# One transformer layer with a mixture of experts on one core: experts that add into the output, a split routing, and a reordered front and attention

## The chip, the core and the metric

The kernel runs on one core of one Trainium2 chip. The core has five engines with a queue of instructions each: TensorE (PE, with its weight loads shown as PEld), VectorE (DVE), ScalarE (ACT), GpSimd (POOL) and SyncE (SP), which here only issues DMAs. The engines wait for each other through semaphores. The metric is the device time of one launch in microseconds; smaller is better.

## The reference

The input is 2048 token numbers. Everything is float32, and the kernel keeps that accuracy by splitting operands of a matmul into an upper and a lower part (`hi`, `lo`) and adding three products.

```python
h = ternary_weights(tok_weight)[x]                       # embedding, T=2048, C=256
# attention: 16 heads, three branches, mixed by a gate over the sequence
a1 = attn(q, k1, v1, causal=True)                        # latent keys and values
idx = top_k(x @ w_imp, 64); sel = x[sort(idx)]           # 64 most important tokens
a2 = attn(q, ks(sel), vs(sel), causal=False)             # selected
a3 = attn(q, kw, vw, causal=True)                        # "window"
h = h + (g0*a1 + g1*a2 + g2*a3) @ w_proj
# experts: E=8, top 2 per token, F=512
logits = layernorm(h) @ router_w.T
w1, w2, i1, i2 = sparsemixer(logits)                     # mask by 2*jitter, softmax, pick
for e in range(8):
    y = (silu(x @ w_gate[e].T) * (x @ w_up[e].T)) @ w_down[e].T
    out = out + dense_w[:, e:e+1] * y
h = h + out
```

## The kernel before

The program is a row of stages, each a block at whose end all engines meet: embed (0 to 121 us), project (to 304), select (to 384), attend (to 2221), mix (to 2345) and experts (to the end).

**Project** runs a list of tasks, `front_tasks()`, merged from several streams so that they alternate. A task has a part on PE and one on DVE or ACT, and for stored results one on ACT (`st_hi`, rounding up, L584), POOL (`st_lo`, the rest, L451) and SP (two stores, L399). A `rank` task compares one block of 128 tokens' importance with all others on DVE (three instructions that read `row_all`, L682 to L685) and counts on PE with 17 matmuls of one column (L505, L508). The third phase holds 16 ranks, the `q` tasks, and `v` and `kn` tasks.

**Select** turns the ranks into 64 one-hot columns (`hot`, DVE L917), gathers the selected tokens by matmuls `U`·`hot` on PE (L846) and projects them (L853). `frs` is the flag times each token's `rstd`, multiplied into the one-hot columns.

**Attend** walks 84 units per head (a unit is 512 queries by 128 keys). Per unit: PE makes scores, DVE adds the mask on diagonal units (L1736), ACT makes `prob` and its rounded form `p_hi`, POOL or DVE subtracts them to `p_lo` (L1418, which engine is set by the list `LO_DVE`), and PE multiplies both with the values four units later (L1599, L1601). PE takes them in the fixed order of units. In heads 0 to 11 preparation for later heads is woven in: tasks `prep` whose products are turned on DVE (L1666, L1676), summed on POOL (`turn_sum`, L1400), rounded up on ACT (L1467) and lowered on POOL (`turn_low`, L1408) or, for one part of a `q` task, on DVE (L1661). The values of the next head are split once per head and kind (ACT, then POOL L1430); `SPLIT_W` says at which unit. `FINISH` says at which units DVE finishes the previous head's output.

**Mix** multiplies the heads' outputs with the projection, adds the residual, takes a layernorm and the router logits, and then routes: two gates on DVE (L2021 to L2044), positions of tokens by scans and matmuls, a one-hot code of each token's slot (L2077 to L2092) and a matmul that inverts it (L1907), giving `slot_tok` (which token lies in a slot) and `slot_w` (its weight). It also writes two accumulators in DRAM: `acc0` with the residual `h1`, `acc1` with zeros.

**Experts** takes 23 tiles of 256 slots. POOL per tile `i`: four `h_lo` subtractions (L2177), after the first two indirect gathers for tile `i+2` (L2159), and at the end two indirect scatters that add the rows of tile `i-1` into `acc0` and `acc1` (L2169). The first scatter of a tile waits for the first of the tile before, the second for the second. Slots with no token point to dummy rows behind the 2048. When all are in, SP loads both accumulators (L2146), DVE adds them (L2326), and SP stores the output (L2149).

## Time and profile before

| | us |
|---|---|
| median of 3 runs | 2634.81 (2633.99 to 2637.43) |
| the profiled execution | 2636.5, its span 2634.8 |
| PE, DVE, POOL, ACT busy | 2237.9, 1877.2, 1758.6, 1720.0 |
| mean granted clock of PE | 0.92 of full speed |
| project, select, attend, mix, experts, end | 183, 80, 1837, 124, 268, 22 |

The times of a stage are read by where one block's instructions end and the next one's begin. "End" is what follows the landing of the last scatter. Of the page's forty slices PE is at 9 tenths in those of attend and lower before and after; the busy share of an engine over the whole span says little about the stages outside attend.

### The profile page before, as it was taken

To read this page: it belongs to the slowest core of one execution; us is meant where nothing else is said; L and a number is where in the kernel's file an instruction comes from. 1 tells how busy PE (TensorE), PEld (TensorE's weight loads), DVE (VectorE), ACT (ScalarE), POOL (GpSimd) and SP (SyncE) were. 2 spreads that over 40 slices of the span, in tenths; PEclk is the share of its full clock that TensorE was granted. 3 is DMA by queue.
4 is the path that set the end of the run, shared out by engine and by line. 5 is a ranking of instruction groups with operands and counts; after the bars stand their busy time and mean duration, and the time that the engine had idled before them with its cause. 6 is when DMAs were issued, how large, how long until landed. Compare 5 with 4: busy or idle time off the path is not lost. (4 is left out here: it accounts for less than half of the span.)

```text
span 2634.8 us, 37397 instructions
## 1 busy us (share of the span) xinstructions
PE 2237.9 (85%) x11394; PEld 1863.9 (71%) x11394; DVE 1877.2 (71%) x3720; ACT 1720.0 (65%) x3574; POOL 1758.6 (67%) x1544
## 2 busy tenths in 40 slices
PE   0178578999999999999999999999999994839885
PEld 0165437887878788787878878788888883728885
DVE  2656467687887878787787878788888873555553
ACT  3433216787877878777787777788888883216663
POOL 4154516778787877878787787877878774017884
PEclk9975569999999999999999999999999997759998
DMA  9767726345252434425342542322412203426776
GB/s 380 327 204 236 224 62 166 75 91 133 62 137 74 93 86 96 119 75 134 77 93 76 107 111 63 94 43 55 80 34 55 44 16 87 140 83 189 194 197 169
DMA packets 199860, 314.81 MB, mean 119 GB/s; under 512 B 95915, under 2 KB 130219, under 8 KB 186731
## 3 DMA queue, kind: packets, MB, share of 16 engines
q1 hardware_dynamic: 189947, 298.23, 40.6%
q0 software_dynamic: 9712, 14.18, 2.9%
q8 instruction: 91, 1.49, 0.2%
q14 instruction: 110, 0.90, 0.1%
HBM read 210.20 MB, written 101.75 MB: 118 GB/s over the span
## 5 line engine op out<-in xcount | busy, mean ns | idle before, releaser
L1418 POOL TENSOR_TENSOR p_lo<-prob,p_hi 128x512 fp32r<-128x512 f32 (+3 forms) x1072 | 1232.6, 1169 | 396.6 <-ACT p_hi L1502 368.4
L1500 ACT ACTIVATE prob<-ps_s 128x512 f32<-128x512 f32 (+4 forms) x1344 | 727.2, 541 | 380.8 <-DVE ps_s L1736 208.8
L1502 ACT ACTIVATE p_hi<-ps_s 128x512 fp32r<-128x512 f32 (+3 forms) x1344 | 726.3, 540 | 1.6
L1634 DVE TENSOR_REDUCE max_part<-ps_x 128x1 f32<-128x512 f32 x744 | 506.7, 687 | 108.5 <-PE ps_x L1546 98.2
L1632 DVE CUSTOM_DVE_ANT_0 ps_x<-ps_x,before 128x128 f32<-128x128 f32 x496 | 244.0, 492 | 30.5 <-PE ps_x L1546 22.0
L1599 PE MATMUL ps_o<-p_hi,v_lat 128*128 128x512 f32 (+3 forms) x640 | 240.3, 376 | 26.0 <-POOL p_lo L1418 25.9
L1599 PE MATMUL ps_o<-p_hi,v_win 128*128 128x512 f32 (+3 forms) x640 | 238.0, 372 | 2.7 <-POOL p_lo L1418 2.7
L1601 PE MATMUL ps_o<-p_lo,v_lat 128*128 128x512 f32 (+3 forms) x640 | 237.8, 372 | 0.0
L1601 PE MATMUL ps_o<-p_lo,v_win 128*128 128x512 f32 (+3 forms) x640 | 235.2, 367 | 0.0
L1418 DVE TENSOR_TENSOR p_lo<-prob,p_hi 128x512 fp32r<-128x512 f32 (+1 forms) x208 | 207.7, 999 | 10.8 <-ACT p_hi L1502 10.7
L1736 DVE TENSOR_TENSOR ps_s<-ps_s,mask_kq 128x128 f32<-128x128 f32 x512 | 150.2, 300 | 74.2 <-PE ps_s L1518 65.6
L1599 PEld LDWEIGHTS ps_o<-p_hi,v_lat 128*128 128x128 f32 x640 | 122.3, 191 | 55.7 <-POOL p_lo L1418 32.9
L1695 DVE TENSOR_TENSOR raw_o<-ps_o,low_sum 32x512 f32<-32x512 f32 x192 | 131.4, 684 | 26.2 <-ACT low_sum L1482 19.7
L1599 PEld LDWEIGHTS ps_o<-p_hi,v_win 128*128 128x128 f32 x640 | 121.5, 190 | 30.3 <-POOL p_lo L1418 8.2
L2159 POOL DMA_INDIRECT xg<-x_scratch,slot_tok x46 | 51.7, 1124 | 130.4 <-POOLq L1755 119.8
L1514 PE MATMUL ps_s<-head_first 97*128 97x512 f32 (+1 forms) x320 | 123.3, 385 | 16.0 <-POOL v_lat L1434 8.2
L1601 PEld LDWEIGHTS ps_o<-p_lo,v_lat 128*128 128x128 f32 x640 | 123.3, 193 | 19.2
L1601 PEld LDWEIGHTS ps_o<-p_lo,v_win 128*128 128x128 f32 x640 | 122.4, 191 | 17.8
L1514 PE MATMUL ps_s<-q_hi,kw_hi 97*128 97x512 f32 (+1 forms) x320 | 121.0, 378 | 6.3 <-ACT p_hi L1502 5.8
L1546 PE MATMUL ps_x<-k_hi,head_first 96*128 96x512 f32 (+2 forms) x320 | 119.3, 373 | 4.1 <-DVE turned L1677 1.8
L1514 PE MATMUL ps_s<-q_hi,k_hi 99*128 99x512 f32 (+1 forms) x320 | 120.0, 375 | 0.3 <-ACT p_hi L1502 0.3
L1517 PE MATMUL ps_s<-head_first,k_hi 96*128 96x512 f32 (+1 forms) x320 | 119.7, 374 | 0.0
(433 smaller groups left out, 5823.6 us busy)
## 6 DMA issues: line engine op xcount, KB each, us to landing
raw<-in_experts_w_dram SPq DMA_DIRECT2D x23, 1536.0 KB
wbuf<-in_tok_weight_dram SPq DMA_DIRECT2D x16, 2000.0 KB, 16.9
head_first<-kw_scratch SPq DMA_DIRECT2D x72, 256.0 KB, 5.0
kw_scratch<-st_hi SPq DMA_DIRECT2D x48, 256.0 KB, 2.3
kw_scratch<-st_lo SPq DMA_DIRECT2D x48, 256.0 KB, 3.0
q_scratch<-st_hi SPq DMA_DIRECT2D x48, 256.0 KB, 4.4
q_scratch<-st_lo SPq DMA_DIRECT2D x48, 256.0 KB, 5.1
head_first<-q_scratch SPq DMA_DIRECT2D x48, 256.0 KB, 6.0
```

Of the source, the lines that this page charges most:

```text
L1418: ns.tensor_tensor(upper if low else p_lo[:, i % LSLOTS, c:CH], prob[low:P, i % NPROB, c:CH], upper.bitcast(F32), ALU.subtract).then_inc(s ...
L1500: nc.scalar.activation(prob[low:P, i % NPROB, c:CH], ps_s[i % 3][low:P, c:CH], ACT.Exp, scale=SCALE).then_inc(s["p_full"], 1)
L1502: nc.scalar.activation(p_hi[:, i % SLOTS, c:CH], ps_s[i % 3][:, c:CH], ACT.Exp, scale=SCALE).then_inc(s["p_up"], 1)
L1514: nc.tensor.matmul(out, hi, xhi, start=True, stop=False)
L1517: nc.tensor.matmul(out, hi[0:rows] if rows else hi, xlo, start=False, stop=False)
L1546: last = nc.tensor.matmul(bank[:, 0:w], q_hi[par][0:DQK, q * P:(q + 1) * P], k_hi[b][par][0:DQK, c * CH:c * CH + w], start=True, stop=True)
L1599: last = nc.tensor.matmul(bank[:, c:CH], w, p_hi[:, i % SLOTS, c:CH], start=(k == 0), stop=bool(low))
L1601: last = nc.tensor.matmul(bank[:, c:CH], w, p_lo[:, i % LSLOTS, c:CH], start=False, stop=output_of(i) is not None)
L1632: ins = nc.vector.tensor_tensor_reduce(bank[:, 0:w], bank[:, 0:w], g.before[:, CH - w:CH], 1.0, -3.0e38, ALU.add, ALU.max, mpart[:, q, c:c ...
L1634: ins = nc.vector.tensor_reduce(mpart[:, q, c:c + 1], bank[:, 0:w], axis=AX.X, op=ALU.max)
L1695: nc.vector.tensor_tensor(raw_o[j * DV:(j + 1) * DV, h % 2, br, :], ps_o[BANK[out]][DV:2 * DV, :], low_sum[64 * (j % 2):64 * (j % 2) + DV, ...
L1736: nc.vector.tensor_tensor(cut, cut, g.mask_kq[:], ALU.add).then_inc(s["cut"], 1)
```

## The change

It has five parts.

1. Project: six ranks move into the second half of the second phase; in the third phase `kn` comes first and the LATENT `v` last. The stores of `lat` are issued before the first `q` instead of the first rank.
2. Select: `hot` is fp32r and made with the flag alone, with one semaphore step per block of tokens, and PE starts with the first; the scale by `rstd` is made by 16 one-column matmuls and applied when the products are copied.
3. Attend: the tables of units below, a `q` part held back by one unit on DVE, two memsets behind the first split.
4. Mix: POOL takes half of both gates; a slot's column comes from rounding instead of 47 comparisons; the weights are inverted in a second pass of matmuls behind `slot_tok`; the first expert loads and gathers are issued inside mix; the zero accumulator is gone and `h1` goes to `out`.
5. Experts: the scatters add into `out`, each behind the landing of the one before it; slots without a token are left out by a bounds check; loads of accumulators, DVE adds and output stores are gone.

```diff
+EARLY = 6
 def front_tasks():
...
-    third = merge([("rank", c, 0) for c in range(NT)], [("q", j, part) for j in range(NJ) for part in range(3)],
-                  values(LATENT) + [("kn", m, j) for m in range(NG) for j in range(NJ)])
-    return first + second + third
+    half = len(second) // 2
+    second = second[:half] + merge(second[half:], ranks[:EARLY])
+    third = merge(ranks[EARLY:] + [None] * 4, [("q", j, part) for j in range(NJ) for part in range(3)] + [None] * 4,
+                  [("kn", m, j) for m in range(NG) for j in range(NJ)] + values(LATENT))
+    return first + second + [t for t in third if t]
...
-            pe.wait_ge(s["hot"], 1)
-            for kc in range(KC):
-                for t in range(NT):
+            for t in range(NT):
+                pe.wait_ge(s["hot"], t + 1)
+                for kc in range(KC):
                     last = nc.tensor.matmul(bank[1 + kc][:, 0:KEEP], g.U[:, t, kc * P:(kc + 1) * P], hot[:, t, :], start=(t == 0), stop=(t == NT - 1))
+            last.then_inc(s["sel"], 1)
+            for t in range(NT):
+                last = nc.tensor.matmul(bank[0][0:KEEP, NT:NT + 1], hot[:, t, :].bitcast(F32), g.rstd[:, t:t + 1], start=(t == 0), stop=(t == NT - 1))
...
-SPLIT_L, SPLIT_W = 20, HU + 16
+SPLIT_L, SPLIT_W = 20, HU + 28
+SUM_LAG, UP_LAG, LOW_LAG = (1, 2), (2, 2, 3), (3, 4, 5)
...
-LO_DVE = sorted(CAUSAL[2::6] + [i for i in range(NU) if UNITS[i][0] == SELECT])
+LO_DVE = sorted([2, 9, 15, 22, 28, 35, 42, 48, 54, 60, 63, 79, 81, 82] + [i for i in range(NU) if UNITS[i][0] == SELECT])
...
-        FINISH = {HU + 6: 0, NU - 8: 1, NU - 6: 2, NU - 5: 3, NU - 4: 4, NU - 2: 5}
+        FINISH = {HU + 6: 0, NU - 16: 1, NU - 14: 2, NU - 11: 3, NU - 8: 4, NU - 5: 5}
...
-            step(nc.vector.tensor_tensor(ge[:], slot[:].unsqueeze(2).to_broadcast([P, N2, NCOL + 1]),
-                                         bound[:].unsqueeze(1).to_broadcast([P, N2, NCOL + 1]), ALU.is_ge))
-            v.add(nc.vector.tensor_reduce(sa[:], ge[:, :, 1:NCOL + 1], axis=AX.X, op=ALU.add))
...
+            step(nc.vector.tensor_scalar(sa[:], slot[:], 1.0 / P, -(P - 1) / (2.0 * P), ALU.mult, ALU.add))
+            step(nc.vector.tensor_scalar(sa[:], sa[:], ROUND, None, ALU.add))
+            step(nc.vector.tensor_scalar(sa[:], sa[:], -ROUND, None, ALU.add))
...
+                    last = nc.tensor.matmul(bank[3][:, 0:NCOL], ohb[:, n, :], vals[:, n, 0, :], start=(n == 0), stop=(n == N2 - 1))
             last.then_inc(s["inv"], 1)
+            pe.wait_ge(s["vals"], 2)
+            for n in range(N2):
+                last = nc.tensor.matmul(bank[4][:, 0:2 * NCOL], ohb[:, n, :], vals[:, n, 1:3, :].rearrange("p k c -> p (k c)"),
+                                        start=(n == 0), stop=(n == N2 - 1))
...
+            sp.wait_ge(s["tiles"], 1)
+            for i in range(2):
+                load_expert(nc, sp, g, a, i)
...
+            pool.wait_ge(s["slots"], 1)
+            pool.wait_ge(s["x2st"], 16 * (NJ + 1))
+            for i in range(2):
+                gather_rows(nc, g, i)
...
-            def scatter(i):
-                pool.wait_ge(s["yw"], HT * (i + 1))
-                for q in range(HT):
-                    n = HT * i + q
-                    if i:
-                        pool.wait_ge(s[f"add{q}"], 16 * i)
-                    nc.gpsimd.indirect_dma_start(out=g.acc_dram[q], out_offset=bass.IndirectOffsetOnAxis(ap=g.slot_tok[:, n:n + 1], axis=0),
-                                                 in_=yw[:, i % 2, q, :], in_offset=None, compute_op=ALU.add).then_inc(s[f"add{q}"], 16)
+            def scatter(i, q):
+                pool.wait_ge(s["yw"], HT * i + q + 1)
+                if i or q:
+                    pool.wait_ge(s[f"add{(q + 1) % HT}"], 16 * (i + q))
+                n = HT * i + q
+                nc.gpsimd.indirect_dma_start(out=out[0], out_offset=bass.IndirectOffsetOnAxis(ap=g.slot_tok[:, n:n + 1], axis=0),
+                                             in_=yw[:, i % 2, q, :], in_offset=None, bounds_check=T - 1, oob_is_err=False,
+                                             compute_op=ALU.add).then_inc(s[f"add{q}"], 16)
...
+                    if f == 2 and i >= 2:
+                        scatter(i - 2, 1)
                 if i:
-                    scatter(i - 1)
-            scatter(NTL - 1)
+                    scatter(i - 1, 0)
+            scatter(NTL - 2, 1)
+            for q in range(HT):
+                scatter(NTL - 1, q)
```

On POOL in the experts before, two tiles in the middle of the stage; `acc0_scratch` and `acc1_scratch` are the two accumulators, `xg` the gathered rows:

```order
909 L2177 TENSOR_TENSOR h_lo<-hm,h_hi 128x256
910 L2159 DMA xg0<-x2_scratch,slot_tok 128x256 x2
911 L2177 TENSOR_TENSOR h_lo<-hm,h_hi 128x256 x3
912 L2169 DMA acc0_scratch<-yw,slot_tok 2176x256
913 L2169 DMA acc1_scratch<-yw,slot_tok 2176x256
914 L2177 TENSOR_TENSOR h_lo<-hm,h_hi 128x256
915 L2159 DMA xg1<-x2_scratch,slot_tok 128x256 x2
```

The same place now; `out_0_dram` is the output:

```order
962 L2235 TENSOR_TENSOR h_lo<-hm,h_hi 128x256
963 L2228 DMA out_0_dram<-yw,slot_tok 2048x256
964 L2235 TENSOR_TENSOR h_lo<-hm,h_hi 128x256
965 L1789 DMA xg1<-x2_scratch,slot_tok 128x256 x2
966 L2235 TENSOR_TENSOR h_lo<-hm,h_hi 128x256 x2
967 L2228 DMA out_0_dram<-yw,slot_tok 2048x256
968 L2235 TENSOR_TENSOR h_lo<-hm,h_hi 128x256
969 L2228 DMA out_0_dram<-yw,slot_tok 2048x256
970 L2235 TENSOR_TENSOR h_lo<-hm,h_hi 128x256
```

The two scatters of a tile stood side by side and aimed at different buffers. Now the third `h_lo` is followed by the second scatter of tile `i-2`, the fourth by the first scatter of tile `i-1`, and both aim at one buffer.

On POOL in the second half of head 1 of attend, before; `full` is a `turn_sum`, `st_lo` a `turn_low`, `v_win` the split of the next head's values:

```order
173 L1418 TENSOR_TENSOR p_lo<-prob,p_hi 128x512 x3
174 L1400 TENSOR_TENSOR full<-turned 128x512 x2
175 L1418 TENSOR_TENSOR p_lo<-prob,p_hi 128x512
176 L1418 TENSOR_TENSOR p_lo<-prob,p_hi 128x384
177 L1408 TENSOR_TENSOR st_lo<-full,st_hi 128x512 x2
178 L1430 TENSOR_TENSOR v_win<-v_win 128x16x32
179 L1418 TENSOR_TENSOR p_lo<-prob,p_hi 128x512 x2
180 L1418 TENSOR_TENSOR p_lo<-prob,p_hi 128x256
181 L1418 TENSOR_TENSOR p_lo<-prob,p_hi 128x512
```

The same place now:

```order
183 L1415 TENSOR_TENSOR full<-turned 128x512
184 L1432 TENSOR_TENSOR p_lo<-prob,p_hi 128x512
185 L1415 TENSOR_TENSOR full<-turned 128x512
186 L1432 TENSOR_TENSOR p_lo<-prob,p_hi 128x384
187 L1432 TENSOR_TENSOR p_lo<-prob,p_hi 128x512
188 L1422 TENSOR_TENSOR st_lo<-full,st_hi 128x512 x2
189 L1432 TENSOR_TENSOR p_lo<-prob,p_hi 128x256
190 L1432 TENSOR_TENSOR p_lo<-prob,p_hi 128x512 x2
191 L1432 TENSOR_TENSOR p_lo<-prob,p_hi 128x128
192 L1432 TENSOR_TENSOR p_lo<-prob,p_hi 128x512 x6
193 L1444 TENSOR_TENSOR v_win<-v_win 128x16x32
194 L1432 TENSOR_TENSOR p_lo<-prob,p_hi 128x512
```

A `turn_sum` of two became two with a lowering between, and the split of `v_win`, which followed the two `st_lo` directly, comes ten lowerings later.

On DVE in mix, before, from the end of the pick of the second gate to its weight; `sm_fac`, `sm_dist` and `sm_keep` are the factor, the distance and the mask of the jitter:

```order
3040 L2026 TENSOR_TENSOR hot<-sm_tie,st_t 128x128
3041 L2028 TENSOR_SCALAR sm_fac<-logit 128x128
3042 L2029 TENSOR_TENSOR sm_fac<-sm_fac,logit 128x128
3043 L2030 TENSOR_TENSOR sm_fac<-sm_fac,st_m 128x128
3044 L2031 TENSOR_TENSOR sm_dist<-st_m,logit 128x128
3045 L2033 TENSOR_SCALAR sm_fac<-sm_fac 128x128
3046 L2034 TENSOR_TENSOR sm_keep<-sm_dist,sm_fac 128x128
3047 L2036 TENSOR_TENSOR sm_tie<-sm_keep,hot 128x128
3048 L2037 TENSOR_TENSOR sm_keep<-sm_keep,sm_tie 128x128
3049 L2039 TENSOR_SCALAR sm_dist<-sm_dist 128x128
3050 L2042 TENSOR_TENSOR sm_keep<-sm_keep,sm_ex 128x128
3051 L2043 TENSOR_REDUCE st_sum<-sm_keep 128x16
```

The same place now, behind the same pick:

```order
3079 L2112 TENSOR_TENSOR hot<-sm_tie,st_t 128x128
3080 L2129 TENSOR_TENSOR r_both<-hot 128x128
3081 L2131 SCALAR_TENSOR_TENSOR r_incl<-r_seg,r_both 128x128
3082 L2132 TENSOR_TENSOR r_excl<-r_incl,r_both 128x128
3083 L2134 COPY r_cnt<-m_ps 128x8
```

The ten instructions on the mask have left the queue, and the scan that numbers the tokens of an expert (`r_incl`) follows the pick at once.

## Rows read from the trace of the kernel before

**Rows 1.** Windows: PE, PEld, DVE, ACT, POOL busy (count), PE clock, DMA share, GB/s.

```profile
180.00:204.00 24.00, 20.79 (x100) 15.31 (x100) 12.52 (x21) 12.16 (x21) 16.19 (x14) 0.99 0.63 191
204.00:288.60 84.60, 68.47 (x392) 42.93 (x392) 60.11 (x65) 33.70 (x59) 46.25 (x33) 0.50 0.75 249
288.60:303.90 15.30, 0.00 (x0) 0.00 (x0) 0.00 (x0) 3.69 (x7) 8.75 (x8) 0.50 0.61 216
520.70:636.80 116.10, 113.53 (x544) 93.65 (x542) 94.64 (x197) 89.66 (x190) 90.76 (x80) 0.99 0.38 91
1790.00:1894.70 104.70, 104.29 (x517) 87.75 (x515) 87.19 (x186) 86.72 (x184) 80.47 (x70) 1.00 0.27 53
2345.30:2612.80 267.50, 219.83 (x1748) 214.56 (x1748) 144.61 (x230) 163.29 (x369) 199.70 (x184) 0.95 0.64 182
2612.80:2634.80 22.00, 0.00 (x0) 0.00 (x0) 4.90 (x4) 0.00 (x0) 0.00 (x0) 0.50 0.87 286
```

**Rows 2.** Windows of the importance row alone: the rank instructions on DVE.

```profile
204.00:288.60 84.60, 49.80 (x47) 0.00 (x0) 0.50 0.75 249
```

**Rows 3.** Waits, 121 to 304 us: waiting instruction, releaser, total, times, longest.

```profile
PE b_ps L505 <- DVEq L687: 15.8, 5, 5.2
```

**Rows 4.** Timeline of PE, 304 to 345 us: start, duration, line, operation, idle before.

```profile
313.08 13.91 PE L846 MATMUL s_ps<-hot,U 128*128 128x64 f32 x64 [7.73 <-DVE hot L917]
327.53 3.65 PE L853 MATMUL s_ps<-wselk,selT 128*64 128x512 f32 x4 [0.54 <-DVE selT L926]
```

**Rows 5.** Waits over ten heads, 520.7 to 1681.1 us.

```profile
PE ps_o L1599 <- POOL p_lo L1418: 23.9, 20, 2.2
DVE st_lo L1661 <- ACT st_hi L1467: 23.5, 10, 2.4
```

**Rows 6.** Timeline of POOL and PE near unit 66 of a head.

```profile
1070.44 2.55 POOL L1408 TENSOR_TENSOR st_lo<-full,st_hi 128x512 fp32r<-128x512 f32 x2
1072.95 1.26 POOL L1430 TENSOR_TENSOR v_win<-v_win 128x512 fp32r<-128x512 f32 x1
...
1075.48 0.50 PE L1599 MATMUL ps_o<-p_hi,v_lat 128*128 128x512 f32 x1 [2.17 <-POOL p_lo L1418]
```

**Rows 7.** Timeline of DVE in the first head.

```profile
418.66 4.46 DVE L1418 TENSOR_TENSOR p_lo<-prob,p_hi 128x512 fp32r<-128x512 f32 x1
```

**Rows 8.** The page's groups: lowering a probability tile on DVE.

```profile
L1418 DVE TENSOR_TENSOR p_lo<-prob,p_hi 128x512 fp32r<-128x512 f32 (+1 forms) x208 | 207.7, 999 | 10.8 <-ACT p_hi L1502 10.7
```

**Rows 9.** Timeline of DVE and PE in the routing of mix.

```profile
2307.60 0.29 DVE L2010 COPY logit<-m_ps 128x128 f32<-128x128 f32 x1 [8.72 <-PE m_ps L1883]
...
2318.98 0.39 DVE L2054 TENSOR_TENSOR r_both<-hot 128x128 f32<-128x128 f32 x1
...
2326.88 1.69 DVE L2079 TENSOR_REDUCE r_sa<-r_ge 128x32 f32<-128x1472 f32 x1
...
2344.38 0.19 DVE L2098 CAST slot_tok<-r_idf 128x46 int32<-128x46 f32 x1
...
2336.70 7.10 PE L1907 MATMUL m_ps<-r_vals,o_hi 128*128 128x138 f32 x32 [15.47 <-DVE o_hi L2092]
```

**Rows 10.** Chain that ended last, at the first gather.

```profile
2347.46 7.37 DMA xg<-x_scratch,slot_tok
```

**Rows 11.** Timeline of POOL over one tile of the experts.

```profile
2457.82 1.62 POOL L2169 DMA_INDIRECT acc_scratch<-yw,slot_tok  x1 [0.66 <-ACT yw L2267]
...
2461.09 1.28 POOL L2177 TENSOR_TENSOR h_lo<-hm,h_hi 128x256 fp32r<-128x256 f32 x1
...
2465.10 1.44 POOL L2177 TENSOR_TENSOR h_lo<-hm,h_hi 128x256 fp32r<-128x256 f32 x2
...
2468.35 1.63 POOL L2169 DMA_INDIRECT acc_scratch<-yw,slot_tok  x1 [0.66 <-ACT yw L2267]
```

**Rows 12.** Chain that ended last, at the last scatters.

```profile
2602.85 3.65 DMA acc_scratch<-yw,slot_tok
...
2607.23 1.54 POOL acc_scratch L2169
```

More of the change, by code:

```diff
@@ L1729, in _ @@
             dve.wait_ge(s["set"], 1)
+            held = [()]
             for h in range(H):
@@ L1736, in _ @@
                         nc.vector.tensor_tensor(cut, cut, g.mask_kq[:], ALU.add).then_inc(s["cut"], 1)
-                    for t in AT.get((h, i), ()):
+                    for t in held.pop(0):
+                        dve_task(dve, t)
+                    tasks = AT.get((h, i), ())
+                    wait = i + 1 < NU and len(tasks) == 1 and tasks[0][0] == "prep" and tasks[0][2] == "q" and tasks[0][4] == 0
+                    held.append(tasks if wait else ())
+                    for t in () if wait else tasks:
                         dve_task(dve, t)
@@ L1772, in mix @@
         x_hi, x_lo = tile("x2T_hi", [P, KC, T], F32R), tile("x2T_lo", [P, KC, T], F32R)
-        sc = {n: tile("sm_" + n, [P, NT, E]) for n in ("rest", "dist", "fac", "keep", "ex", "tie", "order")}
-        top = {n: tile("st_" + n, [P, NT]) for n in ("m1", "m2", "t", "sum")}
+        sc = {n: tile("sm_" + n, [P, NT, E]) for n in ("rest", "dist", "far", "size", "keep0", "keep1", "ban", "ex", "tie", "order")}
+        top = {n: tile("st_" + n, [P, NT]) for n in ("m1", "m2", "t", "t2", "sum")}
         hot = tile("hot12", [P, 2, NT, E])
@@ L2040, in gate @@
[L2040 to L2046 removed]
+                nc.vector.tensor_tensor(best, sc["tie"][:], wide(top["t"][:]), ALU.is_equal).then_inc(s["best"], 1)
@@ L2047, in _, with weigh @@
+                dve.wait_ge(s["best"], n + 1)
+            def weigh(n):
+                dve.wait_ge(s["kept"], n + 1)
+                step(nc.vector.tensor_reduce(top["sum"][:], sc["keep%d" % n][:], axis=AX.X, op=ALU.add))
+                step(nc.vector.reciprocal(w12[:, n, :], top["sum"][:]))
+            gate(logit[:], top["m1"][:], hot[:, 0], 0)
             step(nc.vector.tensor_scalar(sc["rest"][:], hot[:, 0], -3.0e38, None, ALU.mult))
             step(nc.vector.tensor_tensor(sc["rest"][:], sc["rest"][:], logit[:], ALU.add))
-            gate(sc["rest"][:], top["m2"][:], hot[:, 1], w12[:, 1, :], 1, hot[:, 0])
+            gate(sc["rest"][:], top["m2"][:], hot[:, 1], 1)
@@ L2115, in experts @@
         yw = tile("yw", [P, 2, HT, C])
-        fin = [tile(f"fin{q}", [P, NT, C]) for q in range(HT)]
         ps_g = [ctx.enter_context(nc.psum_tensor(f"e_g{i}", [P, CH], F32)) for i in range(2)]
@@ L2322, in _ @@
                     lower_x(i + 1)
-            for j in range(NJ):
-                c = slice(4 * j, 4 * j + 4)
-                dve.wait_ge(s[f"fin{j}"], 16 * HT)
-                nc.vector.tensor_tensor(fin[0][:, c, :], fin[0][:, c, :], fin[1][:, c, :], ALU.add).then_inc(s["sum"], 1)
 class Tiles:
```

291 lines of the change are left out of this document (157 added, 134 removed).

## The prediction

> **What bounds the kernel now.** I read the windows by stage first, since the six stages have different limits. In attend (70% of the time) PE is the bound: a head without preparation takes 104.70 us with PE busy for 104.29, one with it 116.10 with 113.53 [rows 1]. The reader is to see that only the second kind has slack to give. In project's last part PE is busy 68.47 of 84.60 us at half clock, with DVE at 60.11, and the 15.30 us behind it hold no PE and no DVE work at all [rows 1]. In the experts PE is busy 219.83 of 267.50 and POOL 199.70 [rows 1]; there the timeline of POOL decides, not the share: each tile takes 10.53 us from first scatter to first scatter, and the only wait of some size is .66 for ACT [rows 11], so POOL's row of instructions sets the pace. The last 22.00 us, from the last landing to the end, are transfers and four adds [rows 1]. Then come the waits, for project and attend [rows 3, 5], and the chain, for the first gather and the last scatters [rows 10, 12]. Sums are made against the profiled execution, 2636.5 us (span 2634.8); the median, 2634.8, lies 1.7 under it. A difference under 0.2% (5 us) can't be told from none.
>
> **Experts, the scatter chain.** Nothing is removed from POOL in a tile; order and waits change. Before, a scatter waited for one that had started 10 us earlier. Now it waits for the last one. A scatter lands 3.65 us after its start, and the next that needs it starts at 2607.23, that is 4.38 after 2602.85 [rows 12]. The chain has two links per tile. One runs beside work: behind the first scatter of a tile (1.62 us) POOL does an `h_lo`, two gathers and two `h_lo`, from 2461.09 to 2466.54, 5.45 us [rows 11]; 7.1 is more than 4.38, so no wait. The other has only the fourth `h_lo` for cover and costs the whole 4.38. A tile is then 7.1 + 4.38 = 11.5, less up to .5 if that first `h_lo` (1.28, against .72 for one of the two at 2465.10 [rows 11]) shrinks: 11.0 to 11.5, so +.5 to +1.0. What the trace can't show is a scatter started 1.5 us after two gathers. If it starts its packets only behind theirs, it lands later; a gather lands 7.37 after its issue [rows 10], and that is the upper price, below as a rival. I add .1 for it and take +.9 a tile, nearest to the undisturbed row. It holds for about 20 of 23 tiles: **+18 us** (+10 to +40). Queued behind the waiting scatter are `h_lo` and gathers, for which PE waits; that is why it costs the pace and not only slack.
>
> The Trainium skill (DMA: Bandwidth & Descriptors, Anatomy of one DMA — SWDGE) gives about 2.0 us plus bytes by bandwidth per DMA issued from GpSimd, 2.3 for these 128 KB, most of it the receipt of the write. By it the link would be some 1.3 shorter and the term about −8; the row has 3.65, and the measurement decides.
>
> **The end.** Removed: accumulator loads, adds, stores, 22.00 us [rows 1]. Added: when the last tile's rows are ready, the old kernel had one link to run (2602.85, 2607.23); now up to four scatters are in a row, 3 × 4.38 + 3.65 = 16.8, against 2612.8 − 2602.85 = 9.95 before. 22.00 − 6.85 − .5 for the exit: **−15 us** (−18, if the first of the four is already out, to −12).
>
> **Mix.** The start is untouched: DVE still lowers both first outputs before the first residual. Routing: ten of the instructions of each gate leave DVE; two gates took 11.38 us, from 2307.60 to 2318.98 [rows 9], and keep 12 plus two new ones at .29 to .33: 4.7, so −6.7. POOL's half is needed only for the weights, behind `slot_tok`. The comparison over 1,504 elements and its reduce (1.69 [rows 9], the other alike) become three over 32: −2.8. Two products over the same 1,472 elements go behind `slot_tok`: −3.3. So `slot_tok` comes 12.8 earlier, at 2331.6 instead of 2344.38 [rows 9]. But a second pass is added ahead of the block's end: the two products 3.4, 32 matmuls, which by [rows 9] took 7.10 at three times the columns of the first pass and which I leave at that, and the sum of weights .4. The end of mix moves by only −1.8. Gathers and weights are already under way, though. The gather chain of 7.37 [rows 10] is hidden, and PE's first transpose, before at its landing (2354.83), starts when mix is over, near 2344.5: **−10 us** (−12 to −2; if the gathers are held by the stores of `x2`, nothing of it shows before −2).
>
> **Project.** Three instructions a rank cost DVE 49.80/16 = 3.1 us [rows 2]. Six go to the window 180 to 204, where DVE has 11.5 us free and PE 3.2 [rows 1]. It grows by about 12: 18.7 on DVE less the free part, and PE's share of the counts. The third part loses 18.7 of DVE and its share of PE's 15.8 of waiting for ranks [rows 3]. Both parts together have PE work of 89.3 in 108.6, so 19 is the most without a higher clock; I take half, −10. PE's clock was .50 in the third part and .99 before it [rows 1]; a part of the new window could fall to the low one (+5), or a part of the third rise (−15). The tail of 15.30 was the last `kn` and `q` through ACT, POOL and SP one by one; now the last tasks are `v` copies and one store. The loads and the 2 MB store at the kernel's end take 22.00 in a row [rows 1], so I give one store 10: −5. **−15 us** (−35 to 0).
>
> **Select.** PE waited 7.73 for all 16 one-hot blocks and then took 13.91 for 64 instructions [rows 4], two for each of 32 fp32 matmuls. In fp32r, as elsewhere in this kernel, it is one each, and they run while DVE makes the blocks: ready at about 313.6 instead of 327. Against it, 16 fp32 matmuls of one column, 32 instructions at .1 to .22 (13.91/64): 3.2 to 7. **−7 us**, of which I count −6, since the inputs of what follows are loading until then (−9 to 0).
>
> **Attend.** A head with preparation is 11.4 longer. Its 27 more PE records at the .24 of a full one account for 6.4; 5.0 are waits and their wake. One is at unit 66: POOL does two `st_lo` and the split in a row, 3.8 us, and PE waits 2.17 [rows 6]; over ten heads these waits are 23.9 [rows 5]. Another is the `q` part on DVE, which waits 2.4 for ACT once a head [rows 5], ahead of the mask that the scores need. The split is now twelve units later, sums and lows are apart, and that part comes behind the mask. All gone: 10 × 5.0, plus some 5 in heads 0 and 11, −55. What is late next: units 64 to 78 on POOL. The list leaves DVE no unit between 63 and 79, so POOL has 11 lowerings at 1.27, a split and in some heads sums there, about 18.9 us beside 18.5 of PE, and the finishing steps now also lie there. They read two tiles in SBUF on DVE, like L1418, which took 4.46 us instead of .7 while POOL ran without a gap [rows 7] and 1.0 in the mean [rows 8]. A finishing step held for 1 to 2 us is new; a mask queued behind it is late. I give back 2 of the 5: **−32 us** (−55 to −3).
>
> The Trainium skill (SBUF — State Buffer, Who interferes with whom) says that such a DVE instruction and a GpSimd one exclude each other for their whole length. The trace agrees with 4.46. By the rule a gap is always lost when POOL is busy throughout, and the term would be nearer to −15; with it the sum would be 17 higher.
>
> **At nothing** go the accumulator's zero writes (SP issues them, no engine waits), the `lat` stores (SP has gaps there), and the two memsets moved behind the first split: two POOL instructions of the size of that split, 1.26 each [rows 6], with PE waiting for loads next; −2.5 to 0.
>
> **Sum.** 18 − 15 − 10 − 15 − 6 − 32 = −60: 2576.5 of the execution, 2575 as a median.
>
> **Rivals.**
> - *The stalls of attend move.* For it: POOL's 18.9 beside 18.5, and [rows 7]. Against: DVE is busy 94.64 of 116.10 [rows 1], so slack is near. Attend gives −5: −33, 2602.
> - *Both large terms are full.* Attend −52, and the clock of project rises, −30: −95, 2540. Against it: 0.50 through all 84.60 us.
> - *Slower: scatters queue behind gathers.* The second scatter of a tile would land 7.4 after its start [rows 10]; its successor starts 8.1 after it. A tile is 7.1 + 8.1 = 15.2, +4.7 over 20 tiles, +94, while the rest gives −78: +16, 2651. It decides from a landing of 6.6 us. Before, nothing waited for these landings, so no row excludes it; against it, the DMA engines are busy for only .64 of the stage [rows 1], and the scatter would have to be held for its gathers' whole flight, though they start 2.5 us earlier.
> - *The change of order does nothing in project*, since DMA and POOL carry it (DMA .75 [rows 1]): −45, 2590; inside the forecast's own range.
>
> **Chances.** Forecast 0.60 (2555 to 2597), moved stalls 0.22, both full 0.10, slower 0.08. The range takes both sides: 2540 to 2615. Faster 0.90, same 0.03, slower 0.07: the slower rival has a little of its chance inside 5 us of none.
>
> **What would show it.** Scatter to scatter at 11.0 to 11.5 us a tile, with the wait of each tile's first scatter on the landing of the one before it; no stall at unit 66 and heads of 111 to 114 us; `slot_tok` near 12.8 us earlier against the logits; `hot` matmuls ending with the last one-hot block; no DVE add at the end. I am wrong if tiles take over 12.5, or if finishing steps on DVE last over 2 us and PE waits behind them.

## The result

The changed kernel takes 2619.95 us (median of 4 runs, 2618.4 to 2622.03) against 2634.7: a ratio of 0.9944 with a 95% interval of 0.9932 to 0.9957. It is faster by 15 us, 0.6%, where 60 us were forecast. Its profiled execution has a span of 2617.7 us and a mean clock of PE of 0.924. Stage by stage, each from its first instruction to that of the next:

| us | before | forecast change | after | change |
|---|---|---|---|---|
| embed and project | 304.0 | −15 | 310.5 | +6.5 |
| select | 80.2 | −6 | 69.9 | −10.3 |
| attend | 1838.1 | −32 | 1805.4 | −32.7 |
| mix, to the experts' first transpose | 132.6 | −10 | 123.1 | −9.5 |
| from there to the end | 279.9 | +3 (+18 −15) | 308.8 | +28.9 |

Attend and mix came out within 1 us of the forecast, select within 5. Project missed by 21.5 us and the experts by 26.

### The profile page after: what moved, and what is told of

Its sections match the earlier page's. It is cut to its first block and busy times, and to the rows that moved or that the text cites. A ratio compares the mean times of both kernels' runs of the same rounds, so it can differ in the third digit from the quotient of the medians.

```text
span 2617.7 us, 37524 instructions
## 1 busy us (share of the span) xinstructions
PE 2253.6 (86%) x11426; PEld 1884.5 (72%) x11426; DVE 1835.2 (70%) x3718; ACT 1718.1 (66%) x3574; POOL 1753.9 (67%) x1549
## 5 line engine op out<-in xcount | busy, mean ns | idle before, releaser
L1432 POOL TENSOR_TENSOR p_lo<-prob,p_hi 128x512 fp32r<-128x512 f32 (+3 forms) x1056 | 1211.1, 1165 | 376.6 <-ACT p_hi L1517 352.8
L1432 DVE TENSOR_TENSOR p_lo<-prob,p_hi 128x512 fp32r<-128x512 f32 (+1 forms) x224 | 190.3, 849 | 44.3 <-ACT p_hi L1517 38.7
L2228 POOL DMA_INDIRECT out_dram<-yw,slot_tok x46 | 77.9, 1693 | 79.8 <-DMA out_dram<-yw,slot_tok 66.6
L2378 DVE TENSOR_TENSOR hm<-silu,e_u 128x256 f32<-128x256 f32 x92 | 38.5, 418 | 131.2 <-POOL h_lo L2235 73.7
```

The costliest lines, as they stand in the source:

```text
L1432: ns.tensor_tensor(upper if low else p_lo[:, i % LSLOTS, c:CH], prob[low:P, i % NPROB, c:CH], upper.bitcast(F32), ALU.subtract).then_inc(s ...
L2228: nc.gpsimd.indirect_dma_start(out=out[0], out_offset=bass.IndirectOffsetOnAxis(ap=g.slot_tok[:, n:n + 1], axis=0), in_=yw[:, i % 2, q, :] ...
```

## The profile after

The windows of the changed kernel, with the same columns as [rows 1]. The first three are project (its second part, its third, its tail), then a head with preparation, one without, the experts, and what follows the last landing:

```profile
180.00:204.00 24.00, 16.51 (x123) 12.59 (x123) 19.28 (x24) 9.78 (x17) 13.14 (x9) 0.93 0.53 165
204.00:299.70 95.70, 79.19 (x369) 49.60 (x369) 52.56 (x62) 39.95 (x71) 59.81 (x45) 0.53 0.67 229
299.70:310.40 10.70, 0.04 (x2) 0.00 (x0) 0.18 (x1) 0.13 (x1) 0.00 (x0) 0.50 0.87 287
734.90:847.60 112.70, 110.76 (x535) 91.62 (x535) 91.89 (x198) 89.25 (x189) 90.23 (x77) 1.00 0.41 107
1746.70:1852.90 106.20, 105.21 (x515) 87.73 (x515) 84.83 (x188) 86.55 (x183) 78.85 (x68) 1.00 0.26 52
2308.80:2613.90 305.10, 238.94 (x1748) 233.23 (x1748) 147.14 (x230) 164.97 (x369) 195.83 (x180) 0.89 0.47 141
2613.90:2617.70 3.80, 0.00 (x0) 0.00 (x0) 0.00 (x0) 0.00 (x0) 0.00 (x0) 0.50 0.00 0
```

A head with preparation is 112.7 long where it was 116.1, but one without is 106.2 where it was 104.7 [rows 1]. The end shrank from 22.0 to 3.8. The experts hold the same PE instructions in 305.1 us, 238.9 of it busy and at a clock of .89 instead of .95: PE waits more, and its clock falls with it. In project, PE ends at 299.7 instead of 288.6; the tail of 10.7 us where it was 15.3 is what was forecast (10).

PE in select, the `hot` matmuls and what follows (start, duration, idle before):

```profile
317.14 5.33 PE L853 MATMUL s_ps<-hot,U 128*128 128x64 f32 x24 [0.47 <-DVE hot L927]
322.39 3.57 PE L856 MATMUL s_ps<-rstd,hot 128*64 128x1 f32 x32
325.83 3.33 PE L863 MATMUL s_ps<-wselk,selT 128*64 128x512 f32 x4
```

They now run while DVE makes the blocks, 32 instructions in place of 64 [rows 4] (the row shows the last 24; the first 8 ran one block at a time), and the one-column matmuls take 3.57, at the low end of 3.2 to 7. `wselk` starts 15.3 us after the stage does, against 23.5.

DVE and PE in the routing of mix: logits, scan, `slot_tok`, the second pass, the first transpose.

```profile
2272.21 0.29 DVE L2093 COPY logit<-m_ps 128x128 f32<-128x128 f32 x1 [8.72 <-PE m_ps L1958]
...
2277.38 0.39 DVE L2129 TENSOR_TENSOR r_both<-hot 128x128 f32<-128x128 f32 x1
...
2297.33 0.19 DVE L2171 CAST slot_tok<-r_idf 128x46 int32<-128x46 f32 x1
...
2300.78 7.06 PE L1987 MATMUL m_ps<-r_vals,o_hi 128*128 128x92 f32 x32 [4.09 <-DVE r_vals L2173]
...
2308.87 1.09 PE L2254 MATMUL e_t<-ident,xg 128*128 128x128 f32 x4 [1.03 <-PEq L1796]
```

From the logits to `slot_tok` it is 25.1 us where it was 36.8 [rows 9], and the first transpose no longer waits for its gather.

The waits of attend over the same ten heads as in [rows 5]:

```profile
PE ps_o L1619 <- POOL p_lo L1432: 16.4, 30, 1.1
...
DVE st_lo L1680 <- ACT st_hi L1482: 5.1, 10, 0.8
```

PE's wait for POOL fell from 23.9 to 16.4 only, while DVE's wait for ACT went from 23.5 to 5.1. The rest of POOL's backlog is at another place. POOL around unit 78 of a head, and PE there:

```profile
1063.89 1.74 POOL L1444 TENSOR_TENSOR v_win<-v_win 128x512 fp32r<-128x512 f32 x1
1065.60 6.60 POOL L1432 TENSOR_TENSOR p_lo<-prob,p_hi 128x512 fp32r<-128x512 f32 x5
```

```profile
1066.90 0.50 PE L1619 MATMUL ps_o<-p_hi,v_lat 128*128 128x512 f32 x1 [1.07 <-POOL p_lo L1432]
```

Before, the stall was 2.17 at unit 66 [rows 6]; now it is 1.07 at unit 78, behind the split's new place, and heads without preparation, in which PE did not wait for POOL at all, have a stall of up to .7 (3.0 us over three heads).

POOL in the experts over one tile, as in [rows 11]:

```profile
2434.86 1.63 POOL L2228 DMA_INDIRECT out_dram<-yw,slot_tok  x1 [0.74 <-issue]
2435.93 1.32 POOL L2235 TENSOR_TENSOR h_lo<-hm,h_hi 128x256 fp32r<-128x256 f32 x1
2439.59 2.14 POOL L2228 DMA_INDIRECT out_dram<-yw,slot_tok  x1 [2.34 <-DMA out_dram<-yw,slot_tok]
2441.23 1.28 POOL L2235 TENSOR_TENSOR h_lo<-hm,h_hi 128x256 fp32r<-128x256 f32 x1
...
2444.25 0.98 POOL L1789 DMA_INDIRECT xg<-x_scratch,slot_tok  x1 [0.30 <-issue]
2445.25 1.44 POOL L2235 TENSOR_TENSOR h_lo<-hm,h_hi 128x256 fp32r<-128x256 f32 x2
2449.31 1.62 POOL L2228 DMA_INDIRECT out_dram<-yw,slot_tok  x1 [2.62 <-DMA out_dram<-yw,slot_tok]
```

The first of these scatters is the second one of its tile and follows the two gathers; the one at 2439.59 is the first of the next tile and stands in front of the gathers. SP in the same stretch; the first of its two weight loads starts at the time shown:

```profile
2441.03 12.25 SPq L1781 DMA_DIRECT2D raw<-in_experts_w_dram  x2
```

From the scatter at 2434.86 to the next it is 4.73 us; from 2439.59 to 2449.31 it is 9.72, with a wait of 2.62 for the landing, though POOL was busy for most of that time. In the mean over tiles 2 to 20 the two links are 4.72 (3.65 to 5.75) and 7.92, together 12.64. The DMA engines' packets tell why. First from the start of the one scatter for 3.7 us, then from the start of the other for 5.8 us (packets, megabytes, share of 16 engines):

```profile
DMA packets 144, 0.13 MB, mean 35 GB/s; under 512 B 16, under 2 KB 144, under 8 KB 144
...
q0 software_dynamic: 144, 0.13, 31.3%
```

```profile
DMA packets 91, 1.12 MB, mean 193 GB/s; under 512 B 0, under 2 KB 0, under 8 KB 0
...
q1 hardware_dynamic: 89, 1.09, 57.8%
```

In the first stretch the scatter's 128 rows and their semaphore writes are all done; its first packet started 2.2 us after the scatter did. In the second, not one packet of the software queue, which carries the scatter, has started after 5.8 us; 89 packets of the weight load, issued 1.4 us after the scatter, have. The scatter's first packet starts 6.0 us after it, so it was held back for 3.8. All landings on the output (four stores of `h1` by SP among them) and the waits of the stage:

```profile
DMA to landing us min/median/max: 2.7/3.9/8.8
```

```profile
DVE hm L2378 <- POOL h_lo L2235: 73.7, 37, 3.2
...
POOL out_dram L2228 <- DMA out_dram<-yw,slot_tok: 66.6, 31, 3.2
...
PE e_g L2270 <- DVE xt_lo L2366: 48.5, 22, 4.7
```

The same two waits of DVE and PE before:

```profile
DVE hm L2316 <- POOL h_lo L2177: 43.0, 23, 2.1
...
PE e_g L2208 <- DVE xt_lo L2304: 25.5, 21, 3.2
```

The two scatters of a tile fare differently. The second one, behind the gathers, lands after 3.8 us in the median and 4.9 at most. The first one lands after 6.8 in the median and up to 8.8; a weight load starts within 2 us of it, on either side, in nearly every tile. POOL waits 66.6 us for landings. Its `h_lo` come later for it, DVE waits 31 us more for them, and PE waits 23 more for the tokens that DVE lowers behind them.

## The experiments

Barriers keep the stages apart, so one run can hold an edit in several, and each is read from its own stage. Runs a to h are single executions. How well a stage repeats is seen where two kernels share its code: 304.0 and 305.6 us for the old list of tasks in project (before and run c), 1796.7 and 1799.2 for the same attend (runs d and i). Differences of 2 to 3 us in a whole stage are not read; a head of the same code repeats within .1 or .2. A tile's time is the mean over tiles 2 to 20, from first scatter to first scatter: 10.49 us before, 12.64 changed. A head's length runs from its first score matmul to that of the next; 112.8 and 106.2 in the changed kernel, with and without preparation.

### Run a_gate_load

```diff
+                if i >= 3:
+                    sp.wait_ge(s["add0"], 16 * (i - 2))
                 load_expert(nc, sp, g, a, i)
```

Front: `EARLY` taken out, third phase `merge(ranks + [None] * 4, ...)`. Attend: `FINISH` of before.

> The changed kernel with three edits in stages that barriers keep apart. Experts: the weight load of tile i is issued only when the first scatter of tile i-3 has landed. Theory L (a scatter's packets wait behind the 1.5 MB weight load that starts just after it): no scatter lands later than 4.5 us, a tile goes from 12.8 us to 11.2 to 11.6, the experts from 305 us to about 275. Rival R (adding into one buffer, or the length of the chain alone, costs it): a tile stays at 12.5 or more. Project: all 16 ranks back in the third phase, the new order of kn and v kept. Theory E (early ranks push matmuls out of the full clock): project ends at 297 to 300, since the tail of 10.7 us stays; rival K (kn first is what costs): 308 or more. Attend: old FINISH table. If the later finishing steps help, a head with preparation gets longer than 112.8 by 1 or more; if they are what made heads 12 to 14 longer, those go from 106.2 to 104.7.

Measured: 2810.77 us, 22.57 us a tile. That is neither of the two expectations: I had the wait one tile too late. POOL issues that scatter at the end of tile `i-2`, and ACT needs the weights of tile `i` in tile `i-1` already, so load and chain took turns; SP's two loads in the view below start over 20 us apart. The landings can be read all the same: with no load beside them the longest takes 5.5 us (8.8 in the changed kernel), and the first scatter of a tile lands in at most 4.6.

```profile
2516.81 22.82 SPq L1779 DMA_DIRECT2D raw<-in_experts_w_dram  x2
```

```profile
DMA to landing us min/median/max: 2.7/3.9/5.5
```

Project: PE ends at 293.6, the stage at 302.6, between what theories E (297 to 300) and K (308) gave. Heads 113.1 and 106.9: the new `FINISH` is worth .3 and .7 beside the late split.

### Run b_quarter_load

```diff
+    w = 6 * CH if i < 2 else 3 * CH // 2
-    sp.dma_start(g.raw[i % 2][:].rearrange("p b c -> p (b c)"),
-                 a["experts_w"][bass.ds(e, 1)].rearrange("o p c -> (o p) c")).then_inc(g.raw_in[i % 2], 16)
+    sp.dma_start(g.raw[i % 2][:].rearrange("p b c -> p (b c)")[:, 0:w],
+                 a["experts_w"][bass.ds(e, 1), :, 0:w].rearrange("o p c -> (o p) c")).then_inc(g.raw_in[i % 2], 16)
```

Front: third phase in the old order without empty places, six ranks early. Attend: `LO_DVE` of before.

> Experts: from the third tile on only a quarter of each expert's weights is loaded (the rest of the buffer keeps old weights, so that part of the computation is left out). Theory L: the load takes a quarter of the 5 us, scatters land in at most 5 us, a tile takes 11.0 to 11.6 us. Rival R: 12.5 or more as before. Project: early ranks kept, third phase in the old order of v and kn and without the empty places. Theory E: project stays long (PE done after 297) and the tail is the long one of 15, end at 312 or more; rival K: PE done near 288, end near 304. Attend: old LO_DVE table. If the new table is what lengthened heads 12 to 14 they return to 104.7; if it relieved POOL in units 64 to 78, a head with preparation goes from 112.8 to 114 or more.

This kernel leaves out three quarters of the weights from the third tile on, so its output is not that of the layer; only its time is read.

Measured: 11.98 us a tile, over the 11.0 to 11.6 of theory L and under R: the small load gives back .66 of the 2.15 lost, and 1.5 stay. The two links are 5.02 and 6.96, the second now as short as the work beside it. The longest landing is 7.0. Project: PE ends at 298.9, the stage at 317.3, as theory E had it: against the 304.0 and 305.6 of the old list without early ranks, six of them cost about 12 us. Heads about 113.4 and 105.5, so the new `LO_DVE` gives .6 with preparation and costs .7 without, beside the late split.

### Run c_two_accumulators

Experts as before the change (two accumulators, loads, adds, stores at the end), early loads kept; front as before; attend:

```diff
-SUM_LAG, UP_LAG, LOW_LAG = (1, 2), (2, 2, 3), (3, 4, 5)
+SUM_LAG, UP_LAG, LOW_LAG = (1, 1), (2, 2, 2), (3, 3, 3)
-                    wait = i + 1 < NU and len(tasks) == 1 and ...
+                    wait = False
```

> Experts: two accumulators, scatters side by side, loads, adds and stores at the end as in the kernel before; the early loads of the changed kernel stay. Both theories: 10.5 us a tile and 22 us at the end; experts from first transpose to the end 280 us against 309 in the changed kernel. Project: the old list of tasks altogether, ends at 304. Attend: old lags of the sums, the rounding and the lows, and the q part not held back; split, LO_DVE and FINISH new. If these lags carry the gain, a head with preparation goes from 112.8 to 114.5 or more; if the later split carries it, it stays within 0.5 of 112.8.

Measured: 10.52 us a tile, 277.7 from the first transpose to the end (280 expected). Project 305.6, which also tells how well such a stage repeats: the same list of tasks gave 304.0. Heads 115.4 and 106.2: without the lags and the held part 2.6 of the 3.3 us are gone, so the first branch of the expectation holds.

### Run d_pair_into_out

```diff
-                if i or q:
-                    pool.wait_ge(s[f"add{(q + 1) % HT}"], 16 * (i + q))
+                if i and q == 0:
+                    for r in range(HT):
+                        pool.wait_ge(s[f"add{r}"], 16 * i)
...
-                    if f == 2 and i >= 2:
-                        scatter(i - 2, 1)
                 if i:
-                    scatter(i - 1, 0)
-            scatter(NTL - 2, 1)
+                    for q in range(HT):
+                        scatter(i - 1, q)
...
-SPLIT_L, SPLIT_W = 20, HU + 28
+SPLIT_L, SPLIT_W = 20, HU + 16
```

> Experts: the two scatters of a tile side by side into the output, the pair waiting for both of the tile before (rows of one tile are different tokens, so the two need no order). Theory L: as in the kernel before the pair stays out of the weight load, 10.5 us a tile and an end of 4 us, so the experts take 262 to 268 us from the first transpose to the end, total near 2577. Rival R (two adds into one buffer slow each other): over 11.5 a tile. Attend: split of the window values back at HU+16. If the later split carries the gain, a head with preparation goes from 112.8 to 115 or more; if the lags do, it stays within 0.5.

Measured: 2564.92 us (2577 expected; attend was 9 us shorter than in the changed kernel), 10.41 us a tile, 261.4 from the first transpose to the end. Both adds go into one buffer at no cost. The timeline of its POOL, one tile:

```profile
2405.72 1.62 POOL L2229 DMA_INDIRECT out_dram<-yw,slot_tok  x1 [0.83 <-ACT yw L2328]
2407.65 1.56 POOL L2229 DMA_INDIRECT out_dram<-yw,slot_tok  x1 [0.30 <-issue]
...
2416.28 1.63 POOL L2229 DMA_INDIRECT out_dram<-yw,slot_tok  x1 [0.84 <-ACT yw L2328]
```

With the split back at its old place the heads take 112.6 and 104.7, the second branch of the expectation. Beside the new lags and the spread `FINISH`, the late split gave nothing with preparation and cost 1.5 us in each head without.

### Run e_gate_one_earlier

```diff
+                if i >= 4:
+                    sp.wait_ge(s["add0"], 16 * (i - 3))
```

Front: all ranks late, `kn` first, no empty places. Attend: split at HU+16, `wait = False`.

> Experts: order and chain of the changed kernel; the weight load of tile i waits until the first scatter of tile i-4 has landed (one tile earlier than in a_gate_load, where it came so late that the load itself set the pace). Theory L+C (the load costs .7 a tile and the chain by itself 1.5): 11.7 to 12.1 us a tile, no scatter's packets later than 3.9 us after its start. If the load is the whole of it: 10.5 to 11. If it is nothing: 12.6. Project: all ranks late, kn before v, no empty places. If the empty places or their spacing cost the 5.9 us by which PE ended later in a_gate_load than before, PE ends near 288 and the stage near 298; if kn first costs it, PE at 293 and the stage near 302. Attend: split at HU+16 and q part not held; new lags. If holding it back carries the gain, a head with preparation takes 115 (d_pair_into_out: 112.6), if the lags do, 113 or less.

Measured: 13.12 us a tile, so this expectation failed. Holding the load back until one scatter has landed sends it out in front of the other, 1.8 us ahead of it in the median. POOL's timeline shows the second one waited for now:

```profile
2429.83 1.89 POOL L2228 DMA_INDIRECT out_dram<-yw,slot_tok  x1 [0.17 <-issue]
...
2436.73 1.57 POOL L2228 DMA_INDIRECT out_dram<-yw,slot_tok  x1 [4.24 <-DMA out_dram<-yw,slot_tok]
```

That scatter has 6.90 to the next, with a wait of 4.24, where the changed kernel had 4.73. The collision moved to the link with less cover. Project: PE ends at 295.8, the stage at 307.9, later than either branch gave; taking the empty places out made it worse. Heads 113.2 and 104.7: holding the `q` part back is worth .6.

### Run f_pair_chained

The pair side by side as in run d, but with the changed kernel's wait for the scatter just before. Front: `EARLY = 2`. Attend: split at HU+16, old lags, part held.

> Experts: the scatters of a tile side by side, but each behind the landing of the one before, as the changed kernel waits. One link of 4.4 to 5 us takes the place of the .3 between the two: if the chain alone costs, 12.6 to 13 us a tile; if PE's or ACT's slack takes it up, 10.5 to 11.5. Project: 2 early ranks in place of 6. If early ranks cost in proportion, PE ends at 294 to 297 (6: 299.7; none: 293.6). Attend: split at HU+16, q part held, lags of the kernel before. If holding it back carries the gain, a head with preparation takes 113 or less, if the lags do, 115.

Measured: 13.16 us a tile. The timeline of its POOL shows the link in the pair and nothing else:

```profile
2433.53 1.62 POOL L2228 DMA_INDIRECT out_dram<-yw,slot_tok  x1 [0.86 <-ACT yw L2327]
2438.28 1.56 POOL L2228 DMA_INDIRECT out_dram<-yw,slot_tok  x1 [3.13 <-DMA out_dram<-yw,slot_tok]
...
2446.51 1.63 POOL L2228 DMA_INDIRECT out_dram<-yw,slot_tok  x1 [0.86 <-ACT yw L2327]
```

4.75 from scatter to scatter where run d has 1.93; that 2.8 is all of the difference between the two (13.16 − 10.41). Nothing takes it up. Project: PE ends at 293.2, as without early ranks (290.5 to 293.6), the stage at 304.1 (299.5 to 302.6): two early ranks cost little, and not in proportion. Heads 115.8 and 104.7: the lags are worth 3.1. They are what cures the stall of unit 66. The later split with the old lags (run c) leaves PE's waits for POOL at 25.8 us over ten heads, none longer than 1.2: it cuts the stall up and takes little off. PE's waits over ten heads, here with the old lags, then in run d with the new ones:

```profile
PE ps_o L1619 <- POOL p_lo L1432: 28.8, 22, 2.6
```

```profile
PE ps_o L1619 <- POOL p_lo L1432: 9.5, 30, 0.4
```

### Run g_pair_old_lowering

Experts as in d, front as in e, attend with the split at HU+16 and `LO_DVE` of before.

> Experts: pair side by side, waiting only for the tile before, as in d_pair_into_out: 10.4 us a tile, 261 us from the first transpose to the end, again. Project as in e_gate_one_earlier. Attend: split at HU+16, the old LO_DVE table, the rest new. If POOL's relief in units 64 to 78 was needed only for the late split, a head with preparation takes 112.6 or less and heads 12 to 14 104.7; if the new table helps by itself, 113.5 or more.

Measured: 2564.61 us; 10.44 us a tile and 262.3, as in d. Project: PE ends at 294.6, the stage at 306.7. Heads 113.0 and 104.2: the new table is worth .4 with preparation and costs .5 without. In the whole of attend (1796.7 in run d, 1799.6 here) no difference is shown, since run i, with the tables of run d, takes 1799.2.

### Run h_no_early_loads

Loads and gathers of the first two tiles moved from mix back to the experts; scatters as in d; front as in a; split at HU+16 and `FINISH` of before.

> Mix: the first two weight loads and gathers are issued by the experts again, the rest of mix is the changed one. If they are what moved the first transpose forward by 9.6 us against the end of attend, it comes at 130 to 132 us after it (changed kernel 123.1, before 132.6), and the first gate matmul 5 us behind it; if the shorter routing on DVE did it, it stays near 123 to 125. Experts as in d_pair_into_out. Project: all ranks late, with the empty places: repeats a_gate_load, PE 293 to 294. Attend: split at HU+16 and FINISH of the kernel before: if the spread finish helps only with the late split, 112.6 and 104.7; if by itself, .3 to .7 more a head.

Measured: the first transpose comes 132.4 us after attend, the gate matmul 5.0 behind it. Its PE waits for the gather again:

```profile
2325.91 1.12 PE L2248 MATMUL e_t<-ident,xg 128*128 128x128 f32 x4 [10.21 <-DMA xg<-x_scratch,slot_tok]
```

Without the early issue nothing of the 9.5 us is left, and the shorter routing shows only through it. Whether early issue would bring as much behind the old routing, with `slot_tok` 11.7 us later, no run shows. Project: PE ends at 290.5, the stage at 299.5. Heads between 113.0 and 116.1, mostly 115.7, and 105.2: with the split at HU+16 the spread `FINISH` is worth 3 us a head. What PE waits for with the old one is ACT, over ten heads:

```profile
PE ps_s L1530 <- ACT p_hi L1515: 20.8, 10, 2.1
```

In run a, with the same old `FINISH` and the split late, that wait is .3 in all. So the two edits do the same work. Heads with and without preparation, the rest of attend alike:

| us | old `FINISH` | spread `FINISH` |
|---|---|---|
| split at HU+16 | 115.7, 105.2 (h) | 112.6, 104.7 (d) |
| split at HU+28 | 113.1, 106.9 (a) | 112.8, 106.2 (changed kernel) |

### Runs i_combined and j_pair_only

i: pair side by side, front as in a, split at HU+16. j: the pair alone.

> The changed kernel with the three edits that the runs point to: scatters of a tile side by side and waiting only for the tile before; all ranks in the third phase with kn first; the window split back at HU+16. By stage from the runs so far: project ends at 300 to 304, select 70, attend 1797, mix to the first transpose 121 to 123, from there to the end 262. Sum 2552 to 2558 of span, 0.969 to 0.971 of the kernel before.

> The changed kernel with the scatter edit alone. If the serial chain and its meeting with the weight load are all that the experts lost, it is faster than the changed kernel by 308.8 less 261.4, 47 us: 2573, ratio 0.976 to 0.977 of the kernel before; attend as in the changed kernel (112.8 and 106.2 a head). The rival, that something else of the run d_pair_into_out gave the gain, would leave it at 2590 or more.

Measured, medians of five and of four runs: i 2557.34 us, 0.9708 of the kernel before (95% interval 0.9695 to 0.9721); j 2572.61, 0.9763 (0.9748 to 0.9778). Both are as expected. j differs from the changed kernel in the scatters alone and is 47 us faster. By stage i has 301.1, 70.2, 1799.2, 123.3 and 261.9. Windows of i: project's second part, third with its tail, and the experts.

```profile
180.00:204.00 24.00, 21.13 (x97) 15.63 (x96) 11.53 (x19) 11.27 (x20) 15.21 (x13) 0.93 0.59 177
204.00:301.10 97.10, 71.44 (x395) 43.30 (x395) 57.59 (x66) 37.54 (x66) 54.81 (x41) 0.50 0.73 254
...
2293.70:2551.80 258.10, 221.50 (x1748) 215.23 (x1748) 148.63 (x230) 163.26 (x369) 192.98 (x180) 0.96 0.57 167
```

PE is back at a clock of .96 in the experts. j's stage took 266.5 instead of the 261.4 of run d, at 10.65 us a tile, which was not looked into; its heads were those of the changed kernel.

## Why the prediction was wrong

**Experts: the step that failed is the length of a tile, 11.0 to 11.5, taken at 11.4.** It was 12.64, over the 12.5 that was named as the sign of being wrong; against the 10.49 of before, the term was +43 over 20 tiles, not +18. It broke in two places. The link without cover was read in the kernel's tail, 4.38 [rows 12]; between tiles it is 4.72 in the mean. And the other link, which 7.1 us of work were to cover, was not covered: it is 7.92, since its scatter lands up to 8.8 us after its start when a weight load starts beside it. The rival "scatters queue behind gathers" had the length of the late landings nearly right (7.4 against a median of 6.8), but on the wrong scatter and for the wrong reason, and so its tile of 15.2 was far too long. The scatter that follows the gathers lands early (2434.86); the one beside the weight load lands late. The trace of before could not price it, since nothing waited for those landings, but it held a hint that I passed over: a gather lands 7.37 us after its issue [rows 10] where an undisturbed scatter needs 3.65. That the waits are the cause is shown by j, where setting the two scatters side by side without a wait between them gives 47 us back, and by f, where the order of j with the waits put in again costs 2.75 a tile. That the load is part of it is shown by b, where a smaller one gives back .66 of 2.15. How much the chain would cost with a full load apart from it is not shown: 1.5 is an estimate from b, and both gates put the load somewhere worse.

The Trainium skill (DMA: Bandwidth & Descriptors, SWDGE vs HWDGE vs iDMA) says that a DMA engine goes round robin between the queues of GpSimd's and of SP's transfers. The same section has an engine switch only at packet boundaries. If each of the load's rows of 12 KB were a packet in that sense, the scatter should have got a turn early, and the trace shows its first packet only after 6.0 us; how many rows make one, no run shows. The page's 2.3 us for such a DMA, weighed in the prediction, was below every landing seen (2.7 the shortest, of scatters that moved no row).

**The end: right.** −15 was forecast. What follows the last landing shrank by 18.2 (22.0 to 3.8); counted as the forecast did, from the moment the last tile's first rows are ready, the end went from 32.2 to 16.1, −16. The four scatters in a row are in the chain as forecast, but land in 2.7 us each, with 3.5 from start to start, where 3.65 and 4.38 were taken. The DMA packets from one of these starts to the next show why:

```profile
DMA packets 144, 0.00 MB, mean 0 GB/s; under 512 B 144, under 2 KB 144, under 8 KB 144
```

The slots of the last tiles hold no token, and rows out of bounds are not written.

**Project: the step that failed is "I take half, −10".** Six early ranks gave no gain: PE ended at 298.9 to 301.5 in the four kernels that have them, at 290.5 to 293.6 in three that have none and the same third phase otherwise. They lengthened the stage by about 10 us (310.5 to 312.3 against 299.5 to 302.6), and by about 12 in the old order (run b). In the window 180 to 204 PE did 16.51 us of work instead of 20.79 [rows 1], since DVE then had 19.28: I had counted DVE's free time and not that PE takes its tasks in order and waits for each. PE waits 6.2 us for ranks in that window, where it waited for none, and its waits for ranks in the whole stage fell from 15.8 [rows 3] to 11.0 only. What was pushed out of that window, at a clock of .93 to .99, was done behind it at .50 to .53: for the same 492 matmuls PE is busy for 95.7 over both windows, against 92.6 in run i. So I read some 3 of the 8 us by which PE ends later than in run i as clock, the rest as waits; no run takes them apart. The half for the tail was right: −4.6. The order alone (ranks late, `kn` first) ends at 299.5 to 302.6 with the empty places and at 306.7 to 307.9 without; the old one at 304.0 and 305.6. Why the empty places help by 5 us was not taken apart.

**Attend: right in size, in part by luck.** −32 against −32.7. The forecast had three cures, the later split, the lags and the held part, and 5.0 of waits a head of which 2 would come back; 3.3 came of each head with preparation, and 1.5 was lost in each without, which no term had. Unit 66 is cured by the lags (3.1; run f); the later split alone only cuts its stall up (run c). The held part is worth .6, the table .4. The finishing steps were counted as a risk alone, but their spreading is worth 3 with the split at its old place (run h). The later split does the same job a second time: it is worth 2.6 with the old `FINISH`, nothing with the spread one, and costs 1.5 or more in heads without preparation in either case. These shares overlap, so they don't add up. The rival "the stalls move" was right in kind, at POOL and unit 78, but not through DVE: lowering a tile there (`p_lo` on DVE) takes less now (849 ns against 999 in the mean).

**Mix: right.** −9.5 against −10, and `slot_tok` 11.7 earlier against 12.8; the two gates took 5.2 us on DVE instead of 4.7, and the second pass took 7.06 where 7.10 was given. Run h shows that the gain needs the issue inside mix.

**Select: right, a bit small.** −10.3 against −6: the start of the next products, from that of the stage, was 8.2 earlier, and the inputs that I thought would hold it back did not. The other 2.1 were not traced.

## What to carry to other kernels

A wait on a DMA's landing must be priced with the transfers that will be in flight then, not from the quiet end of a trace: look which large load starts within the landing time. Before chaining scatters, ask which of them can touch the same row; the two of one tile never do, since a token has one slot with an expert, and setting them side by side without a wait between them was worth 47 us. Two edits against the same wait can do each other's work: measure each without the other. An engine's free time in a window is not room for new tasks when another engine takes their results in order.

## What was not expected of the hardware

A 1.5 MB load issued 1.4 us after a 128-row scatter kept all of the scatter's packets back until 6.0 us after its start, where they start after 2.2 with no load beside them; the landing took 8.8 instead of 3.9. With a load of a quarter the size the landings reached 7.0 at most, with none 5.5. Two adding scatters into one DRAM buffer, with different rows and 1.93 us apart, cost nothing against two buffers (10.41 and 10.52 us a tile). Scatters with all rows out of bounds land in 2.7 us instead of 3.9. An fp32 matmul of 64 columns shows as two instructions, in fp32r as one, at about the same .22 us each (13.91/64 and 5.33/24) with the clock at half.
